# The gating loop's pick product turned: one-hots as the moving side of 24 matmuls of 512 columns

## The reference, cut to what matters

```python
h = (x_flat @ W_gat).reshape(M, HEADS, NUM_EXPERTS)          # M = 16384 rows of 16 values
a_src = (h * att_src).sum(-1)                                 # 4 values for each row
e = leaky_relu(a_src[src] + a_dst[dst], 0.2)
e_max = segment_max(e, dst); ee = exp(e - e_max[dst])
denom = segment_sum(ee, dst)
msg = h[src] * (ee / denom[dst])[:, :, None]
agg = segment_sum(msg, dst)
```

## Time and profile before

| | |
|---|---|
| median of 3 timed runs | 2964.01 us |
| the profiled execution's own time | 2966.14 us |
| its span, first to last instruction | 2964.0 us |
| PE busy | 1194.9 us (40%) |
| DVE busy | 1996.8 us (67%) |
| ACT busy | 561.5 us (19%) |
| POOL busy | 1948.8 us (66%) |
| mean granted TensorE clock | 0.653 of full speed |

### The profile page before, as it was taken

One profiled execution on the slowest core, in us unless ns is written; L12 is line 12 of the kernel. 1 busy time (PEld: TensorE's weight loads), 2 busy tenths in 40 slices (PEclk: granted clock), 3 DMA queues, 4 the chain that ended last, 5 costly groups with the idle time before them and its releaser, 6 DMA issues.

```text
span 2964.0 us, 33860 instructions
## 1 busy us (share of the span) xinstructions
PE 1194.9 (40%) x12474; PEld 999.6 (34%) x12474; DVE 1996.8 (67%) x3000; ACT 561.5 (19%) x613; POOL 1948.8 (66%) x1768
## 2 busy tenths in 40 slices
PE   4854000000001000101113695989888988850505
PEld 3432000000000000000102353778888888850305
DVE  7788596977776868877744201388888888850535
ACT  1010002222222222222100112122222222210301
POOL 0000777778787878777577677777777777766262
PEclk9976555555555555555555555699999999975557
DMA  9300212222223232322311644121212121211001
GB/s 309 134 0 23 67 38 99 87 91 90 87 82 96 71 106 74 105 84 76 110 27 47 24 122 68 9 36 23 37 24 36 24 36 24 36 10 43 4 13 33
DMA packets 156178, 185.36 MB, mean 63 GB/s; under 512 B 94692, under 2 KB 114854, under 8 KB 150038
## 3 DMA queue, kind: packets, MB, share of 16 engines
q1 hardware_dynamic: 99602, 120.23, 13.5%
q0 software_dynamic: 56352, 62.34, 12.0%
HBM read 96.24 MB, written 86.23 MB: 62 GB/s over the span
## 4 chain that ended last, share of the span: by engine, by line
POOL 50%; issue 19%; DVE 18%; PE 7%; ACT 3%; DMA 2%; SPq 1%; POOLq 0%; DVEq 0%; ACTq 0%
POOL arena L668 47%; DVE arena L1278 12%; PE psum L869 2%; POOL d_adseed L751 2%; POOL d_qseed L692 1%; DVE arena L1550 1%; DVE arena L1569 1%; PE psum L785 1%; PE psum L948 1%; PE psum L960 1%; DVE arena L1281 1%; DVE arena L1553 1%; SPq L504 1%; ACT arena L1108 1%; ACT arena L1123 1%
## 5 line engine op out<-in xcount | busy, mean ns | idle before, releaser
L1278 DVE TENSOR_TENSOR arena<-arena 128x512 f32<-128x512 f32 (+13 forms) x1371 | 1016.7, 780 | 286.7 <-DMA arena<-d_ac,arena 53.2
L668 POOL DMA_INDIRECT arena<-in_kv,arena x640 | 762.7, 1192 | 195.1 <-issue 194.5
L668 POOL DMA_INDIRECT arena<-d_h,arena x668 | 694.4, 1040 | 205.9 <-issue 205.6
L987 PE MATMUL psum<-arena 128*128 128x128 bf16 x10080 | 620.8, 225 | 86.3 <-DVEq L1762 79.0
L785 PE MATMUL psum<-arena 128*128 128x128 f32 (+4 forms) x568 | 117.6, 380 | 1321.1 <-DVEq L1353 1045.3
L987 PEld LDWEIGHTS psum<-arena 128*128 128x128 bf16 x10080 | 606.3, 101 | 92.3 <-DVE arena L1281 79.9
L785 PEld LDWEIGHTS psum<-arena 128*128 128x128 f32 (+4 forms) x568 | 93.3, 200 | 1346.9 <-DVEq L1353 1060.7
L1281 DVE TENSOR_SCALAR arena<-arena 128x512 bf16<-128x512 f16 (+8 forms) x1054 | 340.4, 382 | 76.5 <-ACT arena L1179 23.6
L668 POOL DMA_INDIRECT arena<-d_adst,arena x40 | 54.3, 1358 | 304.6 <-DVEq L1450 292.7
L1278 DVE TENSOR_TENSOR arena<-psum,arena 128x512 f32<-128x512 f32 x137 | 91.8, 680 | 206.0 <-PE psum L948 200.5
L1550 DVE TENSOR_TENSOR_SCAN arena<-psum,arena 128x2048 f32<-128x2048 f32 x20 | 88.5, 4423 | 185.9 <-ACT arena L1111 185.9
(11 more groups left out here) (155 smaller groups left out, 1334.1 us busy)
## 6 DMA issues: line engine op xcount, KB each, us to landing
d_gs<-arena SPq DMA_DIRECT2D x32, 768.0 KB, 7.0
d_as<-arena SPq DMA_DIRECT2D x20, 1152.0 KB, 4.5
d_qseed<-arena SPq DMA_DIRECT2D x5, 4096.0 KB, 29.8
arena<-d_qseed SPq DMA_DIRECT2D x20, 1024.0 KB, 5.9
arena<-d_h,arena POOLq DMA_INDIRECT x668
arena<-in_kv,arena POOLq DMA_INDIRECT x640
d_adseed<-arena SPq DMA_DIRECT2D x1, 4096.0 KB, 29.4
arena<-d_adseed SPq DMA_DIRECT2D x17, 128.0 KB, 3.8
```

What stands on the lines that cost most here:

```text
L668: return pool.indirect_dma_start(out, None, table, bass.IndirectOffsetOnAxis(index[:, t:t + 1], 0))
L987: last = nc.tensor.matmul(ps[2 + turn_of(b, m)][:, k * PICK_W:(k + 1) * PICK_W], pick_hot[turn_of(b, m)][:, t, k * P:(k + 1) * P], h_split ...
L1278: return V.tensor_tensor(o, a_, b_, op)
```

## The change

The pick product is turned. `h_split` becomes the weights and the one-hots of all 4 edges the moving side, so a batch takes 24 matmuls of 512 columns and not 96 of 128. The result then has the 8x16 candidate values on the partitions and the 512 edges along the row, and three new steps bring the right values back to the edges:

- `spread_cands` (PE) and `all_cands` (ACT) lay the candidate number of each edge over all partitions, as `spread` and `all_keys` do with the key.
- `keep_own` (DVE, one instruction) keeps of each column only the 16 partitions of its own candidate: compare with the partition's number, times the PSUM result.
- `sum_cands` (PE) multiplies the kept 128x128 block of each edge column (fp32 weights) by the constant `pick_sum`, 20 columns wide: it sums the candidates and yields 16 values of `h` and 4 of `a_src` at once. `picked_rows` (ACT) copies the 80 columns to `hs`.

`take_picked`, `picked_a_src` and `pick_of` go. `pick_keys` keeps 8 steps, the last a 28-column copy in place of a 224-column compare, but its semaphore now comes behind all 8 and not behind the first 4. `maximum` also waits for `pick_rows_set`, and PE waits for the 14 expert groups ahead of the loop.

```diff
+C_CAND, C_SEL = 840, 841
+C_COLS = 860
+    c[:, C_CAND] = p // G_HF
+    c[p, C_SEL + p % G_HF] = 1.0
...
+            def spread_cands(it, b, m):
+                pe.wait_ge(pick_cand_set, chunk_count(it, b, BATCHES, m + 1))
+                for k in range(BATCH):
+                    last = nc.tensor.matmul(ps[4 + turn_of(b, m)][:, k * P:(k + 1) * P],
+                                            bc(pick_cand_key[b][:, BATCH * m + k:BATCH * m + k + 1], [P, P]), ident16, start=True, stop=True)
+                last.then_inc(pick_cand_spread, 1)
             def pick(it, b, m):
                 pe.wait_ge(pick_hot_set, chunk_count(it, b, BATCHES, m + 3))
-                pe.wait_ge(pick_taken, chunk_count(it, b, BATCHES, m + 1))
+                pe.wait_ge(pick_kept_set, chunk_count(it, b, BATCHES, m + 1))
+                for t in range(K_TILES):
+                    for n in range(SPLITS):
+                        last = nc.tensor.matmul(ps[2 + turn_of(b, m)][:, :], h_split[n][:, t * PICK_W:(t + 1) * PICK_W], pick_hot[turn_of(b, m)][:, t, :],
+                                                start=t == 0 and n == 0, stop=t == K_TILES - 1 and n == SPLITS - 1)
+                last.then_inc(picked, 1)
+            def sum_cands(it, b, m):
+                pe.wait_ge(pick_kept_set, chunk_count(it, b, BATCHES, m + 3))
+                pe.wait_ge(pick_rows_set, chunk_count(it, b, BATCHES, m + 1))
                 for k in range(BATCH):
-                    for t in range(K_TILES):
-                        for n in range(SPLITS):
-                            last = nc.tensor.matmul(ps[2 + turn_of(b, m)][:, k * PICK_W:(k + 1) * PICK_W], pick_hot[turn_of(b, m)][:, t, k * P:(k + 1) * P],
-                                                    h_split[n][:, t * PICK_W:(t + 1) * PICK_W], ...)
-                last.then_inc(picked, 1)
+                    last = nc.tensor.matmul(ps[6 + turn_of(b, m)][:, k * G_ROW:(k + 1) * G_ROW], pick_kept[turn_of(b, m)][:, k * P:(k + 1) * P], pick_sum,
+                                            start=True, stop=True)
+                last.then_inc(pick_summed, 1)
...
                         for m in range(BATCHES - 2):
                             spread(it, b, m + 2)
+                            spread_cands(it, b, m)
                             pick(it, b, m)
+                            if m >= 1:
+                                sum_cands(it, b, m - 1)
                         for m in range(2):
+                            spread_cands(it, b, BATCHES - 2 + m)
                             pick(it, b, BATCHES - 2 + m)
                             with pe.If(it * 2 + (b + 1) < n_all):
                                 spread(it + b, 1 - b, m)
+                            sum_cands(it, b, BATCHES - 3 + m)
+                        sum_cands(it, b, BATCHES - 1)
...
-            def take_picked(it, b, m):
+            def keep_own(it, b, m):
+                turn = turn_of(b, m)
                 dve.wait_ge(picked, chunk_count(it, b, BATCHES, m + 3))
...
+                dve.wait_ge(pick_cand_set, chunk_count(it, b, BATCHES, m + 3))
+                dve.wait_ge(pick_summed, chunk_count(it, b, BATCHES, m + 1))
+                V.scalar_tensor_tensor(pick_kept[turn], pick_cand[turn], const[:, C_CAND:C_CAND + 1], ps[2 + turn][:, :],
+                                       ALU.is_equal, ALU.mult).then_inc(pick_kept_set, 1)
```

More of the change, by code:

```diff
@@ L363, in build @@
         pick_key = [g.take(PICKS // 2, F16) for _ in range(2)]
-        pick_of = [g.take(PICKS * CANDS) for _ in range(2)]
+        pick_cand_key = [g.take(PICKS // 2, F16) for _ in range(2)]
         pick_all = [g.take(BATCH * P // 2, F16) for _ in range(2)]
-        pick_prod = g.take(BATCH * PICK_W)
+        pick_cand = [g.take(BATCH * P // 2, F16) for _ in range(2)]
+        pick_kept = [g.take(BATCH * P) for _ in range(2)]
+        pick_sum = g.take(G_ROW)
         assert g.at <= LIMIT
@@ L433, in build @@
                              "ends_set", "starts_done", "pos_set"))
-        found = [[sem(f"found{k}_{n}") for n in range(4)] for k in range(2)]
+        found = [[sem(f"found{k}_{n}") for n in range((3, 4)[k])] for k in range(2)]
         last_set, last_shifted, cont_set, cont_out = sem("last_set"), sem("last_shifted"), sem("cont_set"), sem("cont_out")
@@ L441, in build @@
         ad_set = sem("ad_set")
[L442 to L444 removed]
+        pick_keys_set, pick_spread, pick_all_set, pick_hot_set, picked, pick_kept_set, dve_keys, h_split_set = (
+            sem(n) for n in ("pick_keys_set", "pick_spread", "pick_all_set", "pick_hot_set", "picked", "pick_kept_set",
+                             "dve_keys", "h_split_set"))
+        pick_cand_spread, pick_cand_set, pick_summed, pick_rows_set = (
+            sem(n) for n in ("pick_cand_spread", "pick_cand_set", "pick_summed", "pick_rows_set"))
         a_idx_in = [sem(f"a_idx_in{b}") for b in range(2)]
@@ L1179, in all_keys, with all_cands, picked_rows @@
                 nc.scalar.copy(pick_all[turn_of(b, m)], ps[turn_of(b, m)][:, 0:BATCH * P]).then_inc(pick_all_set, 1)
+            def all_cands(it, b, m):
+                act.wait_ge(pick_cand_spread, chunk_count(it, b, BATCHES, m + 1))
+                act.wait_ge(pick_kept_set, chunk_count(it, b, BATCHES, m + 1))
+                nc.scalar.copy(pick_cand[turn_of(b, m)], ps[4 + turn_of(b, m)][:, :]).then_inc(pick_cand_set, 1)
+            def picked_rows(it, b, m):
+                act.wait_ge(pick_summed, chunk_count(it, b, BATCHES, m + 3))
+                lo = G_RUN - PICKS + m * BATCH
+                nc.scalar.copy(hs[b][:, lo:lo + BATCH, :],
+                               ps[6 + turn_of(b, m)][:, 0:BATCH * G_ROW].rearrange("p (j f) -> p j f", f=G_ROW)).then_inc(pick_rows_set, 1)
             def gelu(n):
@@ L1195, in _ @@
             act.sem_inc(pick_all_set, 2)
+            act.sem_inc(pick_cand_set, 2)
+            act.sem_inc(pick_rows_set, 2)
             with act.If(n_all >= 3):
@@ L1202, in _ @@
                     with act.If(it * 2 + b < n_all):
[L1203 to L1212, removed]
+                        for m in range(BATCHES - 2):
+                            all_keys(it, b, m + 2)
+                            all_cands(it, b, m)
+                            if m == 1:
+                                lay(it, 1 - b, 1)
+                            if m >= 1:
+                                picked_rows(it, b, m - 1)
+                            if m == 2:
+                                weigh(it, 1 - b, 1)
+                            if m == 3:
+                                rows(it, 1 - b, 1)
+                        for m in range(2):
+                            all_cands(it, b, BATCHES - 2 + m)
+                            with act.If(it * 2 + (b + 1) < n_all):
                                 all_keys(it + b, 1 - b, m)
+                            picked_rows(it, b, BATCHES - 3 + m)
+                        picked_rows(it, b, BATCHES - 1)
                     with act.If(it * 2 + b == n_all):
@@ L1657, in _ @@
             dve.sem_inc(h_split_set, 1)
-            step(V.tensor_copy(ident16, ident))
+            V.tensor_copy(ident16, ident)
+            own = const[:, C_SEL:C_SEL + G_HF]
+            V.tensor_copy(pick_sum[:, 0:G_HF], own)
+            step(tt(pick_kept[0][:, 0:G_HF], own, att[:, 0, :], ALU.mult))
+            step(V.tensor_reduce(pick_sum[:, G_HF:], pick_kept[0][:, 0:G_HF].rearrange("p (h k) -> p h k", k=G_EXP), AX_X, ALU.add))
             dve.sem_inc(h_split_set, 1)
@@ L1695, in maximum @@
                 dve.wait_ge(g_laid, c1)
+                if back:
+                    dve.wait_ge(pick_rows_set, chunk_count(it, 1 - b, BATCHES, 2))
                 link(it, b, back, V.tensor_tensor_scan(ad_edge, g_nst, ad_fm, 0.0, ALU.mult, ALU.add))
@@ L1792, in _ @@
                             one_hot(it, b, m + 2)
-                            take_picked(it, b, m)
+                            keep_own(it, b, m)
                             if m == 1:
```

43 lines of the change are left out of this document (10 added, 33 removed).

## The result

The changed kernel takes 3000.57 us (median of 4 runs, 2996.38 to 3003.96), the kernel before, timed beside it, 2964.11 us (2962.47 to 2969.45). The ratio is 1.0119, 95% interval 1.0099 to 1.0139: 1.2% slower, 36 us. The forecast was 3036 us, 72 us slower, so the direction was right and the size twice too large. The profiled execution took 3003.05 us, its span is 3000.9.

The account below looks back on a forecast made before the run. POOL's gathers were taken to bound the loop, with the PE and DVE chain last after the change. Chain 33.5 + clock 36.5 + second stop 12 - 10.1 spare = 72 us slower, 3036 us; range 2980 to 3078.

Parts of the forecast that it names:

- The chain of PE and DVE ends the loop instead: Gating loop: the new wait makes PE and DVE last, mean 52.2 us a chunk against POOL's 50.4; excess 33.5 us.
- In a chunk that begins with a jump PE's stop of 3.16 us now stands behind sum 6 in the path: Loop jump on PE: the earlier trace's stop joins the path, giving 53.8 us for such a chunk, 2.1 more.
- 33.5 - 10.1: Gating loop: the chain's excess of 33.5 us, less the 10.1 us it had to spare against POOL.
- 50.6 us for a chunk without jump and clock: PE and DVE chain, from one long scan's end to the next: 50.6 us, 3.0 more than 47.7.
- 14 x 2.6 = 36.5: Pick 0 behind PE's stop ahead of sum 6: runs slow at 1.2 GHz in each of 14 chunks, 36.5 us.
- the rival whose clock holds: Gating loop: the chain is last, but PE's stop leaves the clock at full speed; 2987 us, chance 0.17.
- A second stop, 3.4 us, at the edge ... 12: PE from pick 5 to the keys: a 3.4 us stop that may slow the clock; a third of 36, 12 us.
- The sums, 0.45 us a batch: PE's sum_cands: four fp32 matmuls with 128x128 weights, between 0.22 and 0.98 us, taken as 0.45.
- The picks, 5.2: PE's pick of 24 matmuls of 512 columns: costed by columns at 5.2 us a batch, bounds 1.3 and 12.2.
- `keep_own`, 0.68: DVE instruction in place of the multiply: 0.68 us, from a row with the same 512 columns out of PSUM.
- the rival with picks of 3.1 us: PE picks take 3.1 us, so POOL bounds the loop again; 2960 us, within the 0.12 for POOL last.

Follow-up runs that it names:

- e1_keep_first: The changed kernel with DVE's keep_own of batch 6 moved ahead of the next chunk's one-hots of batch 1: 2972.74 us, ratio 1.0036.
- e2_wait_only: The kernel before plus one wait: PE waits at each chunk's end until DVE has taken batch 6 of the picks: 3026.83 us, ratio 1.022.
- e3_narrow: The changed kernel with each 512-column pick matmul cut into four of 128 columns, 96 a batch again: 3025.43 us, ratio 1.0206.
- f8_fill: The changed kernel with 48 unread matmuls filling PE's stop ahead of sum 6, on a third chip: 2979.39 us, ratio 1.0044.
- e7_before_skip: The kernel before with outer conditions around DVE's and PE's gating loop bodies, on a chip where before takes 3846.96 us: 3798.53 us, ratio 0.989.

## Why the prediction was right in direction and wrong in size

The steps, in the prediction's order:

- **"The chain of PE and DVE ends the loop instead": right**, with the stop ahead of sum 6 (2.94 to 3.14 us where 3.5 was said), the 6.78 us ahead of the one-hots of batch 2, and POOL waiting for indices. e1_keep_first takes the stop away and the loop is as fast as before; e2_wait_only adds the wait alone and loses 63 us.
- **"In a chunk that begins with a jump PE's stop of 3.16 us now stands behind sum 6 in the path": the first step that failed.** I took the jump's stop from the earlier trace rows and kept it for a program with a quarter of the matmuls. It goes with the fetching of instructions, and the fetches went with them: the changed kernel shows no stop at the jump. Put back in e3_narrow, it costs 26 us (last scan at 2719.66 for 2693.27), 19.7 of them in the stops themselves; 7 x 3.16 = 22 had been in the sum. Without clock and jump the loop ends 0.5 us earlier than before (f8_fill), and with 26.4 for the jumps that makes 25.9, where this part of the sum had 33.5 - 10.1 = 23.4. The working of the chain itself was right to 2.5 us: it gave 50.6 us for a chunk without jump and clock, and f8_fill measures 50.49.
- **"14 x 2.6 = 36.5" for the clock: too large**, 24 to 26 by f8_fill, and more by what POOL's bound hides. The 2.6 are from a pick with its first 5.4 us or so at half speed. The windows of the kernel before (clock is the third last column):

```profile
2232.40:2236.00 3.60, 3.60 (x35) 3.60 (x36) 3.40 (x10) 0.81 (x2) 2.69 (x4) 0.50 0.65 217
2236.00:2238.00 2.00, 2.00 (x23) 2.00 (x22) 1.67 (x3) 0.00 (x0) 1.69 (x2) 0.55 0.78 124
2238.00:2240.00 2.00, 2.00 (x40) 2.00 (x38) 0.65 (x4) 0.00 (x0) 1.39 (x3) 1.00 0.17 17
```

  And those of the changed kernel around the stop:

```profile
2214.00:2216.50 2.50, 0.00 (x0) 0.00 (x0) 2.49 (x7) 0.00 (x0) 1.89 (x3) 1.00 0.15 10
2216.50:2218.70 2.20, 2.00 (x16) 1.94 (x18) 0.72 (x2) 0.45 (x2) 1.59 (x3) 0.71 0.13 12
2218.70:2220.00 1.30, 1.24 (x3) 0.45 (x3) 0.00 (x0) 1.29 (x2) 0.99 (x2) 0.50 0.17 10
2220.00:2222.00 2.00, 2.00 (x9) 0.84 (x8) 0.00 (x0) 0.85 (x2) 1.40 (x2) 0.80 0.11 8
2222.00:2225.00 3.00, 3.00 (x19) 1.45 (x18) 0.04 (x1) 0.00 (x0) 2.38 (x3) 1.00 0.19 8
```

  While PE stands here, the granted clock is still full. In steps of 0.5 us it is 1.00 up to 2217.0, 0.90 in the next, 0.50 from 2217.5 to 2220.5, 0.69 in the next and then 1.00 again: it drops when sum 6 is nearly done, some 0.9 us after PE's start, and is back within pick 0. In other chunks it falls while PE still stands, and the whole of sum 6 is slow (1.90 us at 2372.41). The Trainium skill, TensorE: Matmul & The Clock Gate, section "The HAM clock gate (the "warmup" mystery)", has half speed as the state that activity lifts. The trace agrees in that, with 5.14 us for the 23 matmuls at full clock and 6.16 where the row begins at 0.50; what it shows beyond it is that the price of a stop is not a fixed 2.6 us but what of the half-speed stretch falls on work in the path. The mean granted clock of 2000 to 2300 was 0.93 before and is 0.94 now: the clock is not lower, it is low at a dearer place.

  That the clock would drop at all was in part luck. The prediction read from the earlier trace rows that it drops after a stop of 3.33 us and not after 3.16, and had it drop because it put the stop at 3.5. The stops are 2.94 to 3.14 us, and all 14 are followed by a slow pick, so that reading fails, and by it the forecast would have been that of the rival whose clock holds (2987). The kernel before had a row against it already, a pick of 7.15 us behind a stop of only 1.96:

```profile
2567.69 7.15 PE L987 MATMUL psum<-arena 128*128 128x128 bf16 x96 [1.96 <-DVEq L1762]
```

- **"A second stop, 3.4 us, at the edge ... 12": wrong.** It is 0.98 us at 2257.26, 1.35 at most, and of the 14 picks behind it one is slow (6.82 us at 2100.82, behind the 1.35). Why it is so much shorter was not tested.
- **The sums, 0.45 us a batch: 0.81** (2236.85 to PE's next row at 2237.66). Each of these fp32 matmuls has two records: the four of a batch stand as x8. The prediction counted the records of the earlier trace rows as whole matmuls. That its upper bound of 0.98 held is luck: it was left at 1.2 GHz, which made up for the halved count. The picks, 5.2: 5.20 (2231.65 to 2236.85); `keep_own`, 0.68: 0.73. That the 24 wide matmuls cost by their columns was right, and the rival with picks of 3.1 us is out.
- **DVE's idle time after the loop had no step at all.** DVE's 81.6 us of "issue" were in the trace of the kernel before and I took the tail as unchanged. It cost 10.3 us, for a reason that has nothing to do with picks: DVE's bodies became shorter.

In one line: 72 forecast, less 22 to 26 for the jumps, less 11 for the clock and 12 for the second stop, 10 more for the empty turns, is 33 to 37; measured were 36. The direction was right by its mechanism, the new wait; the terms that failed are these four.

## What to carry to other kernels

Before a stop that is seen in a trace is carried over to a changed program, ask what it is made of: here the stop of "issue" at PE's jump came and went with the number of instructions between the jumps, together with the instruction packets. A new wait is best judged by what stands ahead of the instruction that ends it: here it was one swap of two independent steps on another engine that decided over 25 to 28 us. And a long "issue" ahead of the first instruction after a loop is worth a look at how many turns the loop makes with nothing to do: one outer condition in DVE's loop and one in PE's gave 41 us, more than the whole change had moved.

## What was not expected of the hardware

- An empty turn of DVE's loop, five jumps and no work, takes 10.2 us and moves five instruction packets of 8 KB; with bodies 24 instructions shorter it takes 11.5, with the same packets. With two jumps (one outer condition) 8 empty turns are over before the 17.6 us that the transfer beside them needs.
- PE's loop body of before is fetched anew in each turn (92 packets in the loop); with a quarter of the matmuls it is not (3 packets), and the jump's stop of 3.16 us is gone.
- Four fp32 matmuls with 128x128 weights and 20 columns take 0.81 us at full clock, 0.20 each, and have eight records.
- PE's 14 stops of 2.94 to 3.14 us each come with a stretch at half speed, which begins in the stop or up to about 1 us behind it, and filling them with work that nobody reads gives back the 24 to 26 us that they cost.
- POOL's indirect gather, 0.95 us otherwise, takes 8.66 us beside a DVE scan of 20x4096 that reads two tiles in SBUF.
- The same kernel takes 2964 and 2968 us on two chips and 3847 us on a third. There PE stops for up to 2.5 us between two matmuls of one pick (e7_before_skip).
